# Attention masks of 8-wide heads written by sixteen 32x32 tiles of the array instead of two rounds of four 64x64 tiles

## The reference

```
scores = einsum('bhqd,bhkd->bhqk', q, k) / sqrt(8)
layer 0: scores = where(abs(query - key) <= 64, scores, -inf)
layer 2: scores = where(mask, scores, finfo.min)     # one 128x128 mask for all sequences and heads
attn = softmax(scores);  out = einsum('bhqk,bhkd->bhqd', attn, v);  out @ Wo.T + bo
```

## Time and profile before

| | us |
|---|---|
| median of three runs | 1955.03 |
| the profiled execution | 1954.56 |
| its span | 1953.0 |
| TensorE matmul busy | 1697.6 (87%) |
| VectorE busy | 1086.3 (56%) |
| ScalarE busy | 890.3 (46%) |
| GpSimd busy | 654.2 (33%) |

### The profile page before, as it was taken

The page is one execution under the profiler, slowest core; times in us unless marked ns, Lnnn a source line. Parts: engine busy times, 40 slices in busy tenths (PEclk is TensorE's granted clock), DMA queues, the critical chain, the costliest instruction groups (busy, mean ns, idle before and its releaser), DMA issues.

```text
span 1953.0 us, 48479 instructions
## 1 busy us (share of the span) xinstructions
PE 1697.6 (87%) x18886; PEld 1241.2 (64%) x18886; DVE 1086.3 (56%) x3147; ACT 890.3 (46%) x2432; POOL 654.2 (33%) x656
## 2 busy tenths in 40 slices
PE   6999974887589999988999926996799999999978
PEld 3666663666468878874666626996466666666753
DVE  6777665677432222125777743665466665665558
ACT  3444311675244544433433305664365555555525
POOL 3332103675311111113235454554133323333315
PEclk9999966787589999999999957998899999999969
DMA  6000001000000000007310011222100000000001
GB/s 182 9 14 8 3 1 32 12 12 1 6 1 1 1 2 1 2 17 290 152 39 24 22 36 51 59 58 76 63 18 1 17 18 17 7 1 1 2 1 44
DMA packets 48828, 63.55 MB, mean 33 GB/s; under 512 B 8106, under 2 KB 37701, under 8 KB 48349
## 3 DMA queue, kind: packets, MB, share of 16 engines
q1 hardware_dynamic: 44253, 51.98, 8.2%
q0 software_dynamic: 4352, 8.47, 1.4%
HBM read 32.29 MB, written 28.65 MB: 31 GB/s over the span
## 4 chain that ended last, share of the span: by engine, by line
PE 57%; issue 10%; DVE 8%; POOLq 3%; POOL 3%; DVEq 2%; ACT 1%; DMA 1%; SPq 1%; PEldq 0%; PEld 0%; ACTq 0%
PE single L1852 5%; PE quad L1840 5%; PE quad L2156 3%; PE single L2173 3%; PE single L652 2%; PE quad L2162 2%; PE pair L1813 2%; PE pair L2536 2%; PE single L2520 2%; PE quad L2571 2%; PE quad L156 1%; PE quad L2562 1%; PE single L2548 1%; PE single L2571 1%; PE pair L1896 1%
## 5 line engine op out<-in xcount | busy, mean ns | idle before, releaser
L2774 POOL TENSOR_TENSOR arena<-arena 128x512 f32<-128x512 f32 x128 | 130.5, 1041 | 297.7 <-DVE arena L2693 297.7
L263 POOL TENSOR_TENSOR rstd<-var_eps,neg_half 128x4 f32<-128x4 f32 (+1 forms) x64 | 66.1, 1032 | 314.8 <-DVE var_eps L259 260.7
L1925 ACT ACTIVATE arena<-quad,arena 128x256 f32<-128x256 f32 x256 | 110.7, 476 | 98.5 <-PE quad L1840 98.5
L909 POOL TENSOR_SCALAR arena<-arena 128x512 f32<-128x512 f32 x56 | 86.9, 1566 | 176.9 <-ACT arena L711 176.9
L2016 DVE TENSOR_TENSOR arena<-single,arena 128x512 f32<-128x512 f32 x32 | 22.1, 692 | 206.6 <-PE single L1852 206.6
L757 ACT ACTIVATE arena<-quad 128x1024 f32<-128x1024 f32 x86 | 86.3, 1023 | 105.7 <-PE pair L636 54.1
L2629 ACT ACTIVATE arena<-pair,arena 128x128 f32<-128x128 f32 x256 | 91.1, 381 | 88.8 <-DVE arena L2688 88.8
L2629 ACT ACTIVATE arena<-quad,arena 128x128 f32<-128x128 f32 x256 | 91.1, 381 | 86.3 <-DVE arena L2688 86.3
L1840 PE MATMUL quad<-arena,wide 128*128 128x256 f32 x512 | 121.6, 385 | 3.1 <-issue 2.2
L1852 PE MATMUL single<-wide,arena 128*64 128x128 f32 x2048 | 123.9, 275 | 0.0
L1852 PEld LDWEIGHTS single<-wide,arena 128*64 128x64 f32 x2048 | 110.7, 137 | 15.7 <-issue 10.0
(11 more groups left out here) (518 smaller groups left out, 4564.6 us busy)
## 6 DMA issues: line engine op xcount, KB each, us to landing
tokens_by_expert<-arena SPq DMA_DIRECT2D x22, 780.0 KB, 8.6
arena<-in_ctxT SPq DMA_DIRECT2D x32, 256.0 KB, 3.0
arena<-tokens_by_expert SPq DMA_DIRECT2D x72, 65.0 KB, 1.8
wide<-in_w SPq DMA_DIRECT2D x2, 2048.0 KB, 10.8
arena<-outputs_by_choice SPq DMA_DIRECT2D x16, 256.0 KB, 4.1
wide<-in_wgu SPq DMA_DIRECT2D x1, 2736.0 KB
x<-in_x SPq DMA_DIRECT2D x4, 512.0 KB, 7.9
out_x<-x SPq DMA_DIRECT2D x8, 256.0 KB, 2.3
```

The costliest lines, as they stand in the source:

```text
L909: mm = pool.tensor_scalar(kv[g % 2][:, :, a, :], kf[g % 2], kmask[:, a:a + 1], None, ALU.mult)
L1925: act.activation(h1T[e % 4][:, f, :], bank[2 + f][:, 0:G * K], ACT.Gelu_apprx_tanh, bias=b1c[:, e, f:f + 1]).then_inc(s["h_evac"], 1)
L2774: pool.tensor_tensor(part, part, inv[t % 3][:, 4 * r:4 * r + 4].unsqueeze(2).broadcast_to([P, 4, P]), ALU.mult).then_inc(s["norm_ready"], 1)
```

## The change

- `mask_four` fills all four banks in one call. It issues sixteen matmuls, each with a 32x32 block of the identity as stationary operand and 32 rows of the mask, repeated to 512 columns, as moving operand. Bank r is filled from row strip r, its partition strip c by column strip c; tile (r, c) reads copy (c - r) mod 4 of the mask.
- So each mask has four copies, turned by 0, 32, 64 and 96 rows. Layer 0: GpSimd makes only the plain band mask; ScalarE makes the other three with 12 copies of 32 rows (`band_turns`), ahead of its wait for the weights, and signals `band_turned`, for which TensorE waits before the first mask. Layer 2: SyncE loads the words of the turned copies in 14 DMAs instead of 6, and VectorE makes 8 biases instead of 4, one a slot in slots 7 to 14 of layer 0; `scale_bias(2)` moves to slot 6.
- In `scores` and `turned` both waits now stand ahead of the one call.
- Layer 3 goes on using `mask_banks` with two copies.

```diff
+        def mask_four(pe, banks, turns):
+            for c in range(4):
+                for r in range(4):
+                    rows = slice(32 * r, 32 * r + 32)
+                    pe.matmul(banks[r][32 * c:32 * c + 32, :], identb[rows, rows],
+                              turns[(c - r) % 4][rows, :].unsqueeze(1).broadcast_to([32, 4, P]), start=True,
+                              stop=False, skip_group_check=True)
...
# load_sync
-                for h in range(2):
-                    sp.dma_start(mask_words[64 * h:64 * h + 64, i, 1, :],
-                                 t["mask2"][i, 64 - 64 * h:128 - 64 * h]).then_inc(w_in[2], 16)
+                for k in range(1, 4):
+                    cut = P - 32 * k
+                    sp.dma_start(mask_words[0:cut, i, k, :], t["mask2"][i, P - cut:P]).then_inc(w_in[2], 16)
+                    sp.dma_start(mask_words[cut:P, i, k, :], t["mask2"][i, 0:P - cut]).then_inc(w_in[2], 16)
...
# load_pool
-            for m in (band, band_other, band_lower):
-                pool.memset(m, 0.0)
+            band = mask_turns[0]["S"][0]
+            pool.memset(band, 0.0)
...
-            keep_where(pool, band_other, 0, 1, -1)
-            keep_where(pool, band_lower, 0, -1, 1)
             pool.drain()
             keep_where(pool, band, 64, 1, -1)
-            pool.drain()
-            pool.tensor_copy(band_other[64:128, :], band_lower[64:128, :])
             pool.drain().then_inc(consts_in, 1)
+        def band_turns(act):
+            turns = mask_turns[0]["S"]
+            for k in range(1, 4):
+                for r in range(4):
+                    f = (r + k) % 4
+                    mm = act.activation(turns[k][32 * r:32 * r + 32, :], turns[0][32 * f:32 * f + 32, :], ACT.Copy)
+            return mm
...
+        def later_mask(dve, i, k):
+            dve.tensor_scalar(mask_turns[2]["ST"[i]][k], mask_words[:, i, k, :].bitcast(U8), -1.0, -NEG, ALU.add, ALU.mult)
...
# scores
-                    mask_banks(pe, [bank_of(m, 0), bank_of(m, 1)], mask_bias[l]["S"])
                     if m == 0:
                         pe.wait_ge(s["k_evac"], 2)
+                        if l == 0:
+                            pe.wait_ge(s["band_turned"], 1)
...
-                    mask_banks(pe, [bank_of(m, 2), bank_of(m, 3)], mask_bias[l]["S"])
+                    mask_four(pe, [bank_of(m, r) for r in range(4)], mask_turns[l]["S"])
...
# turned
-                    mask_banks(pe, [bank_of(n, 0), bank_of(n, 1)], mask_bias[l]["T"])
                     pe.wait_ge(s["s_free"], min(2 * n + 3, 2 * N))
-                    mask_banks(pe, [bank_of(n, 2), bank_of(n, 3)], mask_bias[l]["T"])
+                    mask_four(pe, [bank_of(n, r) for r in range(4)], mask_turns[l]["T"])
...
# scalar
+                act.wait_ge(consts_in, 1)
+                if l == 0:
+                    band_turns(act).then_inc(s["band_turned"], 1)
                 act.wait_ge(w_in[l], 16 * w_loads[l])
-                act.wait_ge(consts_in, 1)
...
# vector
-                    if l == 0 and n == 7:
-                        later_masks(dve)
+                    if l == 0 and n == 6:
+                        scale_bias(dve, 2)
+                    if l == 0 and 7 <= n < 15:
+                        later_mask(dve, (n - 7) // 4, (n - 7) % 4)
```

More of the change, by code:

```diff
@@ L91, in program @@
         neg_half = sb("neg_half", [P, G])
-        mask_bias = {l: {n: [sb(f"mask{n}{l}{half}", [P, P], BF16)[:] for half in ("own", "other")] for n in names}
-                     for l, names in ((0, "S"), (2, "ST"), (3, "S"))}
-        mask_bias[0]["T"] = mask_bias[0]["S"]
-        mask_words = sb("mask_words", [P, 2, 2, P // 4], I32)
+        causal_bias = [sb(f"causal_{half}", [P, P], BF16)[:] for half in ("own", "other")]
+        mask_turns = {l: {n: [sb(f"mask{n}{l}by{32 * k}", [P, P], BF16)[:] for k in range(4)] for n in names}
+                      for l, names in ((0, "S"), (2, "ST"))}
+        mask_turns[0]["T"] = mask_turns[0]["S"]
+        mask_words = sb("mask_words", [P, 2, 4, P // 4], I32)
         aw = {l: {n: sb(f"w{n}{l}", [P, P]) for n in "qkvo"} for l in (0, 2)}
@@ L123, in program @@
         w_in = {l: sem(f"w_in{l}") for l in range(4)}
-        w_loads = {0: 8, 2: 8 + 6}
+        w_loads = {0: 8, 2: 8 + 14}
         setup_v = sem("setup_v")
@@ L223, in load_pool @@
             keep_where(pool, band, 64, -1, 1)
-            keep_where(pool, band_other, 0, 1, -1)
-            keep_where(pool, band_lower, 0, -1, 1)
             pool.drain()
             keep_where(pool, band, 64, 1, -1)
-            pool.drain()
-            pool.tensor_copy(band_other[64:128, :], band_lower[64:128, :])
             pool.drain().then_inc(consts_in, 1)
+        def band_turns(act):
[5 more added lines that the diff above has]
+            return mm
         def later_consts(pool):
-            causal, causal_other = mask_bias[3]["S"]
+            causal, causal_other = causal_bias
             causal_lower = arena.tensor[:, ARENA - 64:ARENA].bitcast(BF16)
@@ L286, in load_dve @@
             scale_bias(dve, 0).then_inc(cols_in, 1)
-        def later_masks(dve):
-            scale_bias(dve, 2)
-            for i, n in enumerate("ST"):
-                for h, m in enumerate(mask_bias[2][n]):
-                    dve.tensor_scalar(m, mask_words[:, i, h, :].bitcast(U8), -1.0, -NEG, ALU.add, ALU.mult)
+        def later_mask(dve, i, k):
+            dve.tensor_scalar(mask_turns[2]["ST"[i]][k], mask_words[:, i, k, :].bitcast(U8), -1.0, -NEG, ALU.add, ALU.mult)
         TILES = 2 * B + E
@@ L424, in small_heads @@
                 "v_mm", "v_evac", "s_ready", "s_free", "mhl_ready", "mt_ready", "mts_ready", "st_ready", "st_free",
-                "pv_ready", "o_free", "o_ready", "x_done", "xb_ready", "stats_ready") + ((
+                "pv_ready", "o_free", "o_ready", "x_done", "xb_ready", "stats_ready",
+                "band_turned") + ((
                 "tables_ready", "c_squared", "rstd_ready", "xr_ready", "rt_ready", "rt_copied", "sel_ready",
@@ L2531, in scores @@
                         pe.wait_ge(s["exp_done"], t - 1)
-                    mask_banks(pe, [S[o][:, r * 512:(r + 1) * 512] for r in range(2)], mask_bias[3]["S"])
+                    mask_banks(pe, [S[o][:, r * 512:(r + 1) * 512] for r in range(2)], causal_bias)
                     for i in range(4):
```

2 lines of the change are left out of this document (removed).

## The result

The changed kernel took 1970.1 us (median of 5 runs, 1965.1 to 1972.3), the kernel before 1953.9 us beside it; the ratio is 1.0074 with a 95% interval of 1.0057 to 1.0090. The forecast, 1946.2 us, had the wrong sign. The profiled execution took 1966.12 us, with a span of 1964.4 us, 11.4 us more than before.

What follows compares the result with a forecast made beforehand. A slot loop of TensorE and VectorE was taken as the bound: 58 x (0.175 - 0.04) = 7.8, less 0.2, gives 7.6 us; 1954.56 - 7.6 - 1.1 = 1945.9, median 1946.2 us; 8-in-10 range 1942 to 1958.

Steps and rivals of the forecast that it cites:

- The S mask: Masks in scores: one call instead of two, starts 3.3 ns apart, first score 0.38 us after the first mask, 0.175 us saved.
- Two rounds: Rival, mask calls: a row strip can't feed four column strips, calls take 0.62 us; 20 us slower, 1974; 6%.
- float32-like starts: Rival, mask calls: starts 6.7 ns apart, so S gains 0.125 and T loses 0.09 us; 1951.9 us; 15%.
- each start costs by itself: Rival, mask calls: starts some 27 ns apart as if tiles gave nothing; 34 us slower, 1988; 3%.
- The T mask: Masks in turned: all start when the maximum ends, 0.38 instead of 0.34 us, so 0.04 us more per call.
- Behind the waiting mask stand L630, L636 and `attend`: T side, behind the wait: named the work held up, whose users are the exponentials and VectorE's normalise; no separate cost given.
- the starts can't be supplied: Rival, first to last start of a call: starts 13.8 ns apart, 10.7 us slower, 1964.6; 8%.
- The clock: TensorE's granted clock: 1.00 and 0.99 in the two small_heads calls; 1.5 us either side allowed for the 243 to 554 us stage.
- The start: Kernel start: ScalarE's table load leaves the path, TensorE starts 1.3 us earlier, 1.1 us gained (0 to 1.3).
- Count and VectorE: Both small_heads calls: 58 gains and losses count, 6 layer 2 slots are VectorE's; common slot 6.62 instead of 6.76 us.
- The mask biases: VectorE, layer 0: four more biases 0.13 us apart, hidden by idle time at no cost; 1 us if that cover were gone.

Runs made afterwards that it cites:

- e1: Changed kernel with the two waits ahead of the T masks swapped, so the late one rides on a weight load: 1954.59 us, 0.9991 of the kernel before.
- e10: Changed kernel with the late wait carried and layer 2's fills spread two a slot: 1951.89 us, 0.9967 of the kernel before.
- e13: Changed kernel with the late wait carried, fills spread, and dead mask work in the first long waits: 1948.13 us, 0.9953 of the kernel before.
- e9: Kernel before plus a second, already satisfied wait in turned, so the late wait stands alone; no mask_four: 1971.07 us, 1.0062.
- e5: Changed kernel with SyncE's layer 2 fills spread, two a slot instead of six at once: 1961.95 us, 1.0028 of the kernel before.
- e2_third: Second rerun of the changed kernel with mask_four in scores only, T filled by two mask_banks calls: 1943.63 us, 0.9966 of the kernel before.
- e4: Kernel before with each mask matmul split into two of 256 columns, as many as the changed kernel issues: 1958.63 us, 1.0017.
- e11: mask_four in scores only, plus dead mask work in the first long waits of each small_heads call: 1935.61 us, 0.9930 of the kernel before.
- e11_again: Rerun of mask_four in scores only with dead mask work in the first long waits: 1943.36 us, 0.9933 of the kernel before.
- e12: mask_four in scores only, dead mask work in the first long waits, and layer 2's fills spread two a slot: 1934.39 us, 0.9924 of the kernel before.
- e14: Kernel before with dead mask work in the first long waits of each call and nothing else: 1949.9 us, 0.9967.
- e2_s_only: Changed kernel with mask_four in scores only; turned fills its banks by two mask_banks calls: 1946.6 us, 0.9951 of the kernel before.
- e3: Kernel before with one 4-column ScalarE copy ahead of its wait for the weights, so the table loads early: 1955.28 us, 0.9995.
- e2_again: First rerun of the changed kernel with mask_four in scores only, T filled by two mask_banks calls: 1950.81 us, 0.9955 of the kernel before.

## Why the prediction was wrong, point by point

**The S mask (right).** Saved: 0.556 to 0.364, 0.19 us against 0.175. The starts are 3.3 ns apart; all sixteen tiles run at once. "Two rounds", "float32-like starts" and "each start costs by itself" are out. By the Trainium skill, TensorE: Matmul & The Clock Gate, section on packing small matmuls, the sixteen starts would span some 0.06 us, an estimate from its 4 ns for each further tile; the trace has 0.05, so the rule holds here within the resolution. The Trainium skill, TensorEngine Tiling (Array Packing), section on performance considerations, speaks of some 60 cycles of overhead for every matmul. As a price of each start, which is what the rival made of it, the trace doesn't bear it out; how long a single short matmul takes, no run here shows.

**The T mask (the step that failed).** "It starts when the maximum ends, as its second half does now, and costs 0.38 instead of 0.34 us: 0.04 us more." It cost 0.12. With the late wait carried (e1, e10, e13) it costs 0.03, close to the sum's 0.04; the other 0.09 is the lone wait's, which e9 shows by itself. I counted what the moved wait holds up and not in what form it would be issued. Over 58 calls that term turns a gain of 7.8 into 58 x (0.19 - 0.12) = 4 us.

**"Behind the waiting mask stand L630, L636 and `attend`"** was the second half of the same step: I named who waits, and priced them at nothing. The price is that of dry stretches: 4.43 us in layer 2, up to 1.3 us in other places. Shown: the hole of over 4 us is there in both profiles of the changed kernel, it is 1.58 us when the other wait stands alone (e1), and it goes when the fills are spread (e5). The kernel before has none of 0.6 us in the two calls, and gets two with the lone wait and nothing else (e9). Stretches up to 2.0 us also stand in kernels whose late wait is carried (2.02 us at 897.7 in e2_third). Sixteen halved masks in its place cost little (e4). Shown as well is what ends them: 32 of 34 end 1.2 to 1.6 us after a 16 KB packet of the instruction queue has landed, so TensorE then stands for its next instructions, by all signs. The packet in the big hole took 0.88 us, no longer than others; it started late, when the fills' queue, 91.9% busy until then, had fallen to 18.6%. Argued and not shown is why a lone late wait makes such packets late: while it stands in the sequencer, what is behind it may not be made ready, so that TensorE starts `attend` with little in hand. The queue's row has 155 packets with 2.54 MB, 16 KB each. The Trainium skill, Runtime: NRT & Kernel Launch, section on instruction fetch mechanics, says that each engine fetches such blocks ahead by a DMA queue of its own and that the cost of crossing into one is mostly hidden. The trace of the kernel before agrees with that in the two calls; that of the changed kernel doesn't at 925.7 us, where TensorE stood for 4.43 us until a block had come.

**The rivals.** "Two rounds after all" (6%, 1974 us) gave the nearest time, and "the starts can't be supplied" (8%, 1964.6) the next, both by luck. The one wanted calls of 0.62 us, and they take 0.36. The other's place was the stretch from a call's first start to its last, and only five T calls show a gap there, of 0.1 to 0.4 us. No rival had the wait.

**The clock.** The price of the stage from 243 to 554 us I let vary, and that stage hardly changed (0.71 and 0.72). That the clock of the two calls would stay up I took from rows 2 without a word. It fell at both starts, at 23.2 us for 6.8 us and at 886.7 for 13.7, where the kernel before has 3.4 us at 889.6. In periods that is 5.68 to 7.26 and 5.68 to 8.43. The wait ahead of the first fall, 2.55 us, is as long in the kernel before, so it isn't enough by itself; of the later ones, that for the first T mask of layer 2 grew from 0.71 to 1.22 us. In the five profiles with filled waits (e11, e11_again, e12, e13, e14) it doesn't fall near 24 us; e13 has a fall at 39.7. The early first mask stays a suspect. Of the fifteen profiles that leave the wait ahead of the second scores unfilled, eleven have their first mask at 17.3 to 19.0 us, and in ten of them the clock falls between 22 and 25 us (e4 is the exception). In the four with a first mask at 19.3 to 19.7 us (before, e9, e2_s_only, e2_third) it doesn't. That is a pattern and no cause: e3, which has the early start and nothing else, speaks for the early mask, but in e2 the same code stands on both sides. Whether a run has the fall isn't fixed by the code (e2_again and e2_third).

**The start.** 1.1 us forecast, 0.65 came through to the first maximum, and the low clock took it back (2.4 us in the first two periods). The table load stands at 0.79 us, not at 3.6, since no wait holds it. The twelve copies lie 0.32 us apart, not 0.28, and end at 7.1, still before the `vcol` at 10.14; the first matmul is at 10.68, not 10.3. ScalarE and the start of TensorE, changed kernel:

```profile
0.79 1.28 ACT L243 ACT_TABLE_LOAD   x1 [0.79 <-PEq L2912]
3.25 3.81 ACT L243 ACTIVATE maskS0by<-maskS0by 32x128 bf16<-32x128 bf16 x12 [1.18 <-POOLq L235]
10.14 0.40 ACT L757 ACTIVATE arena<-ident,acol 128x128 f32<-128x128 f32 x1 [3.08 <-DVE acol L295]
...
22.93 0.51 PE L166 MATMUL quad<-maskS0by,identb 32*32 32x512 bf16 x16 [2.55 <-DVE arena L801]
```

**Count and VectorE (right).** With the wait carried the common slot is 6.59, and VectorE's late slots hardly moved (7.88 and 8.75 beside 7.87 and 8.75 before, then 7.87 and 9.14 beside 7.90 and 8.79). The eight DMAs more show nowhere in the periods. The mask biases, one a slot now, may show in one: the tenth period of layer 0 is 6.82 us in the changed kernel and 6.81 in e2_s_only, where its neighbours have 6.57, and there VectorE, with statistics and a bias to make, starts the maximum without idle time before it. The prediction had said that idle time hides the biases in such slots; here it costs 0.24 us at most.

**Open.** What decides from run to run whether the clock falls; why e14 gained 5 us; why a block of instructions starts late after a lone wait and beside the fills; and why the masks give 6.6 of the 11 us on the S side: a few slots (8.12, 7.59 in e11_again) with dry stretches of about 1 us hold most of the difference.

## What to carry to other kernels

Idle time by "issue" in the middle of a run of matmuls is a sign that the next instructions came late; look for a packet of the instruction queue that landed just before its end. When an edit puts two waits ahead of one instruction, look in the sequencer's rows which of them stands alone, and write the late one first, so that it is the one carried; here that order is worth 0.8%. Shortening work beside a wait is a saving only while the engine still has work in hand and the clock stays up: price a longer wait at the start of a stage by a possible fall of the clock, and try filling it with dead matmuls (0.33% on the kernel before; with the S masks 0.9930 against 0.9966, e11 beside e2_third). Merge only the side whose work stands in the chain; on the other side, half of the masks were free under the maximum and worth keeping there.

## What the runs showed of the hardware

- Two waits ahead of one weight load: one is an instruction of 51 ns in the sequencer, and if it is the late one, the work behind it starts 0.09 us later (0.487 against 0.394 us in e9, 0.515 against 0.423 in e1).
- Sixteen 32x32 tiles in bf16 with 512 columns start within 0.05 us, and the next kind of matmul starts 0.37 us after the first, against 0.555 for eight 64x64 tiles in two rounds.
- TensorE can stand for 4.4 us although its work waits for nothing that the profile shows. Such stretches end 1.2 to 1.6 us after a 16 KB packet of the instruction queue has landed (32 of 34 of 0.6 us or more in the two calls, all runs).
- The granted clock fell to the lower level (1.2 of 2.4 GHz; 0.60 on average over 16 us of e2_again) for 3.4 to 13.7 us near the start of a call. A fall of 3.4 us cost 1.4 us of a call's periods (first period of layer 2, 5.56 before and 4.18 in e14), one of 13.7 us 5.0 us (layer 0, 209.1 in e2_again and 204.1 in e2_s_only).
